# Reordering the first routing's matrix work and splitting the first gathers over a block boundary

## The reference, cut to what matters

```python
x = x + 0.5 * ffn(layernorm(x))       # expert layer 1
x = x + attention(layernorm(x))       # memory attention, scan over 8 chunks of 128 positions
x = x + 0.5 * ffn(layernorm(x))       # expert layer 2

def ffn(tokens):                      # E = 8 experts, F = 1024, CAP = 320 tokens for each expert
    logits = tokens @ gate_w          # 256 x 8
    probs = softmax(logits); expert = argmax(probs)
    pos = cumsum(one_hot(expert)) - 1 # place of a token in its expert's list; over CAP it is dropped
    h = relu(expert_input @ w1)       # 256 x 1024 per expert
    return combine(h @ w2, probs)     # 1024 x 256 per expert
```

## Time and profile before

| | us |
|---|---|
| three runs | 764.88, 765.0, 766.89 |
| median of the runs | 765.0 |
| profiled execution, first to last instruction | 767.1 |
| PE busy | 673.5 (88%) |
| DVE busy | 606.4 (79%) |
| ACT busy | 438.1 (57%) |
| POOL busy | 240.0 (31%) |

### The profile page before, as it was taken

One profiled execution on the slowest core, in us unless ns is written; L12 is line 12 of the kernel. 1 busy time (PEld: TensorE's weight loads), 2 busy tenths in 40 slices (PEclk: granted clock), 3 DMA queues, 4 the chain that ended last, 5 costly groups with the idle time before them and its releaser, 6 DMA issues. The chain is left out here.

```text
span 767.1 us, 15489 instructions
## 1 busy us (share of the span) xinstructions
PE 673.5 (88%) x5715; PEld 580.6 (76%) x5715; DVE 606.4 (79%) x1373; ACT 438.1 (57%) x1105; POOL 240.0 (31%) x201
## 2 busy tenths in 40 slices
PE   5719999999597889999999999999998469999996
PEld 2218899898476777988879888887976257989985
DVE  0677788773488999999999999999985869887851
ACT  1325575662367667677666877767463446557550
POOL 0023453123311416052350714416061053722202
PEclk9958999999899999999999999999999769999999
DMA  9949637170411004013040311302103715834301
GB/s 343 411 176 349 221 117 254 36 214 22 126 54 56 1 1 141 27 56 112 21 146 1 105 63 56 112 1 77 35 12 100 274 49 166 281 100 163 130 15 35
DMA packets 58226, 89.26 MB, mean 116 GB/s; under 512 B 6960, under 2 KB 49072, under 8 KB 58032
## 3 DMA queue, kind: packets, MB, share of 16 engines
q1 hardware_dynamic: 46176, 70.28, 26.5%
q0 software_dynamic: 3840, 10.49, 4.2%
q10 hardware_dynamic: 8144, 7.61, 3.2%
HBM read 74.73 MB, written 22.02 MB: 126 GB/s over the span
## 5 line engine op out<-in xcount | busy, mean ns | idle before, releaser
L721 PE MATMUL ps<-moe_normedT_high,weights_high_up 128*128 128x320 f32 x252 | 80.8, 321 | 0.4 <-DVE moe_hidden_low L539 0.2
L722 PE MATMUL ps<-moe_normedT_low,weights_high_up 128*128 128x320 f32 x252 | 78.1, 310 | 0.0
L723 PE MATMUL ps<-moe_normedT_high,weights_low_up 128*128 128x320 f32 x252 | 78.1, 310 | 0.0
L1233 POOL TENSOR_TENSOR att_o_rs<-att_o_mean,minus_half 128x4 f32<-128x4 f32 x16 | 16.2, 1013 | 194.7 <-DVE att_o_mean L1491 194.7
L721 PE MATMUL ps<-weights_high_down,moe_hidden_high 128*128 128x256 f32 x256 | 73.3, 286 | 1.0 <-DVE weights_rows L547 1.0
L539 DVE SCALAR_TENSOR_TENSOR moe_hidden_low<-ps,moe_hidden_high 128x256 fp32r<-128x256 f32 x128 | 53.9, 421 | 24.3 <-ACT moe_hidden_high L676 20.2
L723 PE MATMUL ps<-weights_high_down,moe_hidden_low 128*128 128x256 f32 x256 | 71.4, 279 | 0.0
L722 PE MATMUL ps<-weights_low_down,moe_hidden_high 128*128 128x256 f32 x256 | 71.3, 279 | 0.0
L635 ACT CAST weights_high_down<-weights_raw_down 128x256 fp32r<-128x256 f32 x96 | 35.1, 407 | 38.9 <-PE ps L723 32.7
L721 PEld LDWEIGHTS ps<-weights_high_down,moe_hidden_high 128*128 128x128 f32 x256 | 48.1, 188 | 4.3 <-issue 4.3
L315 DVE TENSOR_TENSOR weights_low_down<-weights_raw_down,weights_high_down 128x256 fp32r<-128x256 f32 x128 | 49.8, 415 | 0.0
(11 more groups left out here) (328 smaller groups left out, 2073.6 us busy)
## 6 DMA issues: line engine op xcount, KB each, us to landing
weights_raw_up<-in_w SPq DMA_DIRECT2D x16, 1024.0 KB, 9.3
weights_raw_down<-in_w SPq DMA_DIRECT2D x16, 1024.0 KB, 8.3
first_xt<-in_xT SPq DMA_DIRECT2D x8, 1024.0 KB, 7.7
weights_rows<-x SPq DMA_DIRECT2D x8, 1024.0 KB, 5.6
out_x<-weights_rows SPq DMA_DIRECT2D x8, 1024.0 KB, 4.5
weights_rows<-x ACTq DMA_DIRECT2D x7, 1024.0 KB, 5.6
weights_rows<-x SPq DMA_DIRECT2D x2, 512.0 KB, 4.2
weights_raw_up<-in_w_x SPq DMA_DIRECT2D x1, 768.0 KB
```

The costliest lines, as they stand in the source:

```text
L721: mm(dst, high_l, high_r, start=start, stop=False)
L722: mm(dst, high_l, low_r, start=False, stop=False)
L723: return mm(dst, low_l, high_r, start=False, stop=stop)
L1233: g.tensor_tensor(o_rs[:, n], o_mean[:, n], t["minus_half"][:, n], ALU.pow).then_inc(o_rs_ready, 1)
```

## The change

PE's order in the first routing becomes product i+1, then place i, within each half; the first product of the second half is issued before the first half's `count`. The first block's POOL issues the gathers of row tiles 0 to 2 alone. Tile 3's gather is the first thing POOL does in the expert block, and tile 4's comes after `power_of` for tiles 0 to 2. As `experts` serves both layers, layer 2's tile 4 is issued after that `power_of` too.

```diff
+FIRST_TILES = range(0, 3)
...
-    def gather(self, g):
-        for i in range(PT):
+    def gather(self, g, tiles=range(PT)):
+        for i in tiles:
...
-    FIRST = TILES[1].stop
+    FIRST = FIRST_TILES.stop
...
             if not gathers_made:
-                weights.gather(0)
+                weights.gather(0, FIRST_TILES)
+            weights.gather(0, range(FIRST, PT - 1))
             power_of(0, slice(0, FIRST))
+            weights.gather(0, range(PT - 1, PT))
             power_of(1, slice(FIRST, PT))
...
             pool.wait_ge(router.index_ready, 1)
-            weights.gather(0)
+            weights.gather(0, FIRST_TILES)
...
-            place(0)
-            for i in range(1, GROUPS):
-                products(i)
-                place(i)
-                if i == PER:
-                    router.count(pe, 0)
+            for q in range(BLOCKS):
+                for i in range(PER * q, PER * (q + 1) - 1):
+                    products(i + 1)
+                    place(i)
+                place(PER * (q + 1) - 1)
+                if q + 1 < BLOCKS:
+                    products(PER * (q + 1))
+                    router.count(pe, q)
             router.tabulate(pe, 0)
```

## The result

The changed kernel takes 770.59 us (median of 4 runs, 770.32 to 771.16) against 764.94 for the kernel before on the same chip (4 runs, 763.22 to 766.89). The ratio is 1.0066 with a 95% interval of 1.0037 to 1.0095: slower by 5.0 to 5.7 us, where "no change" was forecast, and above the range.

A forecast was written before the change was run, and what follows sets the result against it. PE's order, DVE and loads were taken to bound the first routing, POOL the block boundary, DMA and POOL narrowly near 88 us. -2.6 + 1.5 + 1.7 + 0.3 = +0.9 on 765.0 gave 766 us, range 761.5 to 768.3.

The forecast's parts named there:

- Steps 1 to 3: First routing's second half 3.7 us earlier, expert block's start 6.1 us earlier, layer 1's L768 5.1 us earlier.
- Step 4: Layer 1: pair 1's last gather lands with or after the copy; POOL restarts at 78.6, 2.6 us earlier (0.8 to 5.1).
- Rival A: Layer 1: pair 1's gathers get through despite the copy, POOL restarts at about 76, kernel takes 761.8 us; chance 0.27.
- Step 5: Layer 1 near 88 us: PE's clock falls after a stand of 3.8 us; 1.5 us lost, bounds 0 and 2.3.
- Step 6: Layer 2's head: tile 4's gather lands later, 1.7 us, and the clock returns later, 0.3; loss 2.0, lower bound 1.4.
- The clock's term: Layer 2's head: PE's emptier stretch makes the clock come back later; 0.3 us, bounds 0 and 1.5.
- the sum's last line: Whole kernel: the runs' median, 2.1 us below the profile's 767.1, is carried over; 765.0 + 0.9, rounded 766 us.
- steps 1 to 5: Layer 1 as a whole: 2.6 us gained at POOL's restart less 1.5 lost to the clock, net 1.1 us gained.
- rival B: Layer 1: the copy's end sets pair 1, POOL restarts only 0.8 to 1.1 us earlier, kernel takes 767.8 us; chance 0.28.

The follow-up runs named there:

- number 5: The changed kernel again, no edit: 770.76 us, ratio 1.0065 to the kernel before.
- number 4: The changed kernel, but SP issues the second half of the copy of x only when pair 1's five gathers have landed: 767.08 us, ratio 1.0013.
- number 8: The kernel before, with only layer 2's tile 4 gather moved behind the power of tiles 0 to 2: 769.04 us, ratio 1.0039.
- number 2: The changed kernel, but layer 2 issues its five gathers together ahead of the first power, as before: 768.08 us, ratio 1.0028.
- number 1: The kernel before again, no edit: 766.66 us, ratio 1.0008; its profiled run took 763.87 us.
- 3: The kernel before with PE's new order in the first routing alone, all five gathers in the first block: 762.83 us, ratio 0.9960.
- 6: The changed kernel with PE's old order in the first routing, the gathers still split: 771.53 us, ratio 1.0067.
- number 7: The changed kernel, but in layer 1 SP waits only for tiles 0 to 2 before issuing pair 1's weights and the copy: 772.10 us, ratio 1.0071.
- number 9: The kernel before with PE's new order, and POOL does pair 1's power ahead of pair 2's five gathers: 779.26 us, ratio 1.0097.
- numbers 9 to 11: Pair 1's power ahead of pair 2's gathers, in the kernels of 3, the changed kernel and number 2: ratios 1.0097, 1.0096, 1.0087.

## Why the prediction was wrong

**Steps 1 to 3** came within 0.7 us: 18.42 for 18.65, 29.39 for 30.05, the block at 50.28 for 49.7, L773 at 58.37 for 58.0, 8.1 us behind the block's start for 8.3. In number 5 the block began at 50.86. The moments were right; what they gained was counted against a slow execution, as shown below.

**Step 4** came at 79.03 for 78.6, `normalise` at 86.62 for 86.2, PE's stand at 2.90 + 1.02 = 3.9 us for 3.8. The cause it gave, the copy, was shown by number 4. One part of it was wrong and did no harm to the number: two or three of pair 1's gathers were to pass ahead of the copy's packets, but the copy was issued at 57.20, before the first of them (58.17), and that one took 16.1 us. PE stood in two pieces and not in one, and in number 5 for only 2.1 us. Rival A is refuted: the gathers didn't get through. The Trainium skill (DMA: Bandwidth & Descriptors, "Queues, rings and completion order") has a DMA engine take turns between queues packet by packet; as rival A used that rule, the trace disagrees: 16.1 us for the gather where 2.8 is its time alone.

**Step 5**: the clock fell where it was expected, for 1.35 us of work (1.5). But number 8 shows that the kernel before can lose as much at that place, so it is no pure cost of the change. **Step 6** was too small: 2.0 in the sum, 2.8 (number 2) and 3.6 (number 8) measured. Tile 4's delay was nearly right: from the first gather to the product that waits are 13.1 us for 11.2, 1.9 for the 1.7 of the sum. The clock's term, 0.3 with an upper bound of 1.5, was mis-sized: PE worked some 4.4 us at the lower clock from that product on (630.0 to 634.4) and 2.6 before (628.8 to 631.4), and half of the difference is 0.9. Such pairs scatter, though: the stretch at the lower clock behind that product is 3.1 to 5.2 us in the seven traces with tile 4 late (mean 3.9) and 0 to 3.6 in the seven without (mean 1.4). Half of the difference of the means is an estimate of 1.2, and with the 1.9 it gives 3.1, between what numbers 2 and 8 measured.

**The step that failed is the sum's last line.** "The runs' median is 2.1 lower than that span; I carry the difference over" took the 2.1 us for something constant around every execution. It is not: in all later profiles the run's own time is 1.7 to 1.9 us **above** the span (770.32 for 768.5, 763.87 for 762.1). By that, the profiled execution of before took about 768.9 us, 3.9 above the median of 765. The unchanged code gave 762.8 to 771.1 in later runs, so it stands near their upper end. Its excess sits in what the change touches: products of 634 ns in the first routing, and weights issued at 56.60 instead of the 53.14 of numbers 1 and 8. So the gains were gains over an execution that had much of the same loss already, and the subtraction of 2.1 then took from the forecast what the median does not lose.

In place of the 2.6 us gained in step 4, the restart comes later than in the other two executions of the old first layer: by 3.2 us against number 1 (75.86) and by 1.4 against number 8 (77.60). At pair 2's `normalise`, behind the clock's loss, the changed kernel's 117.98 stands against 113.79 and 116.77: 4.2 and 1.2 us lost. The ratios say the same over many runs: layer 1 costs 2.1 us (number 2, 0.5 to 3.8) where steps 1 to 5 had a net gain of 1.1, and layer 2 costs 2.8 to 3.6 where step 6 had 2.0. Together that is 4.9 to 5.7 us, and 5.0 to 5.7 were measured; the lower sum must fit, as both its terms come from number 2's ratio, and only number 8's 3.6 is independent of it.

Redoing the sum on number 1's profile alone gives 2.9 + 1.35 + 2.8 = 7.1 us above its 763.87, that is 770.9 for the 770.59 measured. That it fits is luck: its base is 2.8 us below its own median, and its layer 1 loss of 4.3 is twice what number 2 measured.

With hindsight rival B is the nearest: it named the direction and what sets pair 1. But its condition, a restart moved by less than about 1.5 us, wasn't met against the profile (2.1), and its 767.8 was 2.8 too low, as it too was added up on the 765. What couples the gathers to SP is a plain rule of this kernel: POOL restarts 21.8 to 24.6 us after SP's issue of pair 1's weights, in number 1 (22.7), 2 (21.8), 3 (21.9), 5 (22.2), 6 (22.1), 7 (23.5), 8 (24.5), before (24.6) and after (22.8), and 20.6 to 22.7 us after the issue of the copy, whether `gather(1)` starts 2 us after the weights' issue (numbers 2 and 5) or 13 (number 7). The split makes SP wait for tile 4, whose gather comes last and behind `power_of`. It brings everything in the block forward except the one thing that bounds it.

Two things are left partly open. One is why executions of one kernel differ: its runs spread from 763.4 to 771.1. The traces show two places, the first routing, where PE's higher speed comes late or never, and layer 1's first pair, where the clock is lost in number 8 and not in number 1; what decides either isn't shown. The other is why PE's order alone gains 3.1 us where its own stage gains about 1. In its profile SP's loads come 1.3 us earlier than in numbers 1 and 8, the restart 2.1 and 3.8 us earlier, PE doesn't stand and the clock stays full, and pair 2's `normalise` is at 112.31 for 113.79 and 116.77. That fits a kernel which is kept away from the point where PE stands, but three traces don't prove it.

## What to carry to other kernels

Before working out a sum on a profile, place its execution among the runs: set the run's own time beside the span, and if the profile is far from the median, look in the edited stage for what is slow in it. That holds for the profile used to explain a result as well: one of unchanged code is worth two. For a bound made of "issue, then land behind something", ask of each edit when it moves the **issue** of the blocker, and what the issuer waits for; an earlier consumer gains nothing. And an edit in a function that serves two places has to be priced at both: here the place that was not meant cost at least as much (2.8 us and more) as the one that was (about 2).

## What the runs showed of the hardware

- The granted clock printed for the first stage can't be trusted: it reads 1.00 from 4 to 34 us in the profile before, where all eight groups of products took 1.94 us, and 1.00 up to 20 us in number 1, where the same group took 1.94 us at 11 us and 1.07 at 19. The durations tell it.
- A gather of 128 rows that lands in 2.8 us alone took 16.1 issued 1 us after a copy of 4 MB; tile 3's, issued together with the loads, and tile 4's, 1.2 us behind the copy's issue, kept DVE waiting for 3.0 and 4.6 us (number 7).
- PE, DVE and ACT stood together from about 101.5 to 107.3 us while POOL issued ten indirect transfers in a row (number 9; PE waited 6.5, 7.2 and 6.4 us in numbers 9 to 11), with `remote` as the releaser of ACT's wait. The cause is open. All three ran on the one chip whose traces have such waits.
- The same kernel ran 1.1% slower on that chip than on the others (median 773.99, runs from 766.7 to 779.8, against medians of 765.4 to 765.9).
